# Two state space layers of a decoder: rows packed over all partitions, B and C by a block-diagonal product, half of one convolution on TensorE

## The reference

```
h = gelu(x @ w_down.T + b_down); xmid = h                     # 1024 -> 128
def _hydra(u):                                                # run twice
    zxbcdt = u @ in_w.T                                       # 256 z, 288 xBC, 8 dt
    xBC = silu(causal_conv(xBC, 7 taps) + conv_b)             # 256 xs, 16 B, 16 C
    dt_fw, dt_bw = softplus(dt[:4] + bias), softplus(flip(dt[4:]) + bias)
    y_fw = scan(x, dt_fw, A, B, C); y_bw = flip(scan(flip ...))   # 4 heads of 64, state 16
    y = shift(y_fw) + shift(y_bw) + xs * repeat(xs @ fcD_w.T + D)
    yz = y * silu(z)
    return (yz * rsqrt(mean(yz**2) + 1e-5) * norm_w) @ out_w.T
```

## Time and profile before

| | us |
|---|---|
| median of three runs | 3789.64 |
| lowest, highest | 3786.74, 3790.0 |
| the profiled execution | 3786.36 |
| its span, first to last instruction | 3784.4 |
| layer 1 in the span | 64.5 to 238.6 |
| layer 2 in the span | 238.6 to 412.6 |

### The profile page before, as it was taken

How to read it: one execution, slowest core, us unless ns; L and a number is a source line. 1 busy time by engine, 2 the same in 40 slices (tenths; PEclk the granted TensorE clock), 3 DMA queues, 4 the chain that set the end, 5 groups by cost and what they waited for, 6 DMA issues and landing times. The chain is left out here.

```text
span 3784.4 us, 106734 instructions
## 1 busy us (share of the span) xinstructions
PE 3154.1 (83%) x43205; PEld 2143.6 (57%) x43282; DVE 2080.5 (55%) x4831; ACT 1561.5 (41%) x3966; POOL 284.9 (8%) x990
## 2 busy tenths in 40 slices
PE   7555679666599999999598999999999999997698
PEld 4434255333376766666254677767666777674344
DVE  2756667677555555555221555555555555555454
ACT  2212245455322222222211566666666666663433
POOL 1000110000000000000100000000000000001232
PEclk9575889878799999999799999999999999999899
DMA  2000020200100000000101333333333333330100
GB/s 102 3 0 3 6 50 10 92 0 0 47 1 0 0 0 0 0 0 0 56 20 36 87 91 91 90 89 89 91 91 92 91 92 89 89 91 27 69 33 39
DMA packets 278662, 175.64 MB, mean 46 GB/s; under 512 B 14470, under 2 KB 267990, under 8 KB 278540
## 3 DMA queue, kind: packets, MB, share of 16 engines
q1 hardware_dynamic: 275852, 171.68, 15.4%
q0 software_dynamic: 2752, 3.18, 0.5%
HBM read 164.09 MB, written 13.90 MB: 47 GB/s over the span
## 5 line engine op out<-in xcount | busy, mean ns | idle before, releaser
L1845 PE MATMUL ps<-de_hg,st_at 128*32 128x128 f32 x16384 | 516.2, 275 | 0.3 <-DVE st_at L2007 0.3
L1845 PEld LDWEIGHTS ps<-de_hg,st_at 128*32 128x32 f32 x16384 | 424.4, 110 | 31.6 <-DVE st_at L2007 0.5
L1910 ACT ACTIVATE st_th<-ps,st_sw 128x128 f32<-128x128 f32 x1024 | 291.9, 368 | 237.2 <-PE ps L1817 237.2
L1990 DVE TENSOR_TENSOR st_th<-ps,st_sw 128x512 f32<-128x512 f32 x256 | 177.0, 692 | 163.3 <-PE ps L1817 163.3
L1257 PEld LDWEIGHTS ps<-sa_xt,w_wq 128*128 128x128 f32 x2048 | 234.1, 193 | 11.0 <-issue 9.2
L1257 PE MATMUL ps<-sa_xt,w_wq 128*128 128x128 f32 x2048 | 237.3, 277 | 1.9 <-ACT sa_xt L1373 1.9
L1328 PE MATMUL ps<-sa_wo,sa_ct 128*128 128x512 f32 x512 | 226.4, 600 | 13.2 <-issue 13.2
L1806 PE MATMUL ps<-st_hk,st_cwt 112*32 112x128 f32 x4096 | 164.7, 278 | 82.4 <-DMA st_hk<-padded_alignments 79.1
L1817 PE MATMUL ps<-st_fs,st_waf 32*128 32x128 f32 x4096 | 186.5, 296 | 16.1
L2268 PE MATMUL ps<-rf_wb,rf_sp 128*128 128x512 bf16 x737 | 175.4, 385 | 16.9 <-DVEq L2399 15.3
L1806 PEld LDWEIGHTS ps<-st_hk,st_cwt 112*32 112x32 f32 x4096 | 100.2, 109 | 147.5 <-ACT st_gt L1929 93.6
(11 more groups left out here) (384 smaller groups left out, 5911.8 us busy)
## 6 DMA issues: line engine op xcount, KB each, us to landing
st_hk<-padded_alignments SPq DMA_DIRECT2D x254, 448.0 KB, 3.6
X<-in_x_dram SPq DMA_DIRECT2D x16, 512.0 KB, 9.0
out_dram<-X SPq DMA_DIRECT2D x16, 512.0 KB, 2.7
w_wq<-in_Wq_perm_dram SPq DMA_DIRECT2D x1, 4096.0 KB
sa_wo<-in_Wo_perm_dram SPq DMA_DIRECT2D x1, 4096.0 KB, 14.4
gate_inputs<-dp_ro SPq DMA_DIRECT2D x16, 256.0 KB, 2.3
st_rin<-gate_inputs SPq DMA_DIRECT2D x128, 32.0 KB, 3.3
rf_wf<-in_weightT_dram SPq DMA_DIRECT2D x8, 512.0 KB, 8.1
```

What stands on the lines that cost most here:

```text
L1845: ins = pe.matmul(R[g][32 * q:32 * q + 32, :], at[g][:, b, :], hg[:, BG * g + b, q * P:(q + 1) * P], start=False, stop=(b == BG - 1), tile ...
L1910: ins = act.activation(th[g][:, b, :], sums(g, 0)[:, b // 2, (b % 2) * P:(b % 2 + 1) * P], ACT.Tanh, bias=sw[g][:, b:b + 1])
L1990: dve.tensor_tensor(th[g][:, 4:8, :].rearrange("p (k s) n -> p k s n", s=2), sums(g, 1).rearrange("p k (s n) -> p k s n", s=2), sw[g][:, 4 ...
```

## The change

The layer is rewritten; the result is the same function.

- dt and B/C are projected with 32 weight columns each, chunk c into partitions 32c to 32c+32 of one bank, so both occupy 128 partitions by 512 tokens. The B/C convolution reads PSUM directly; dt is copied out once, turned by four transposes, and its first two VectorE operations stand in the middle of the B/C convolution.
- The order of projection is channel tiles 0 and 1, two units of convolution, then z. `pre` holds both tiles.
- Channel tile 1: tokens 1024 to 2047 are convolved on TensorE (`convolve`), seven products per 512 tokens with `taps`, a diagonal matrix per tap; ScalarE adds the bias in its silu. VectorE convolves tokens 0 to 1023.
- B and C go to memory (4 DMAs) and come back (16 DMAs of 256 pieces of 64 bytes) as `bexp`, block-diagonal in the 8 rows of a group, and `cexp`, padded to 18 steps. One product of 18 columns per group gives C against B already reduced; the masked reduction of step 4 is gone.
- The transposes and skip sums run in chunks of 512; the skip sums, like the sums of squares, use 32 columns each at partition 32c.
- Four buffers of `pp`. The norm is done once per layer: sums of squares of the four chunks in one bank, one square root, one reciprocal, and a product with `sel` that spreads a row to all partitions. Output projections are copied to `pre` meanwhile.
- Ahead of the loop: memsets of `sel`, `bexp`, `cexp`, seven products that build `taps`, and six more small DMAs for the repeated convolution weights.

```diff
+                        for c in range(CH):
+                            sp.dma_start(dram_bc[:, c * CW:(c + 1) * CW], bc[32 * c:32 * c + 32, :]).then_inc(bc_out, 16)
+                        sp.wait_ge(bc_out, layer * 16 * CH + 16 * CH)
+                        for r in range(GRP):
+                            sp.dma_start(bexp[of, :, SEQ * r:SEQ * r + SEQ], rows[r, 0:DST], ...
+                            sp.dma_start(cexp[of, :, 1:SEQ + 1], rows[r, DST:2 * DST], ...
...
+                def convolve(pe, layer, n):
+                    pe.wait_ge(projd, layer * UNITS + 2 * CH)
+                    for d in range(TAPS):
+                        ins = pe.matmul(out[:, :, d:], taps[:, TAPS - 1 - d, :], src[:, :, 0:SEQ - d],
+                                        start=(d == 0), stop=(d == TAPS - 1))
...
-                        for g in range(NG):
-                            ins = pe.matmul(ps[:, 4, g * 8:(g + 1) * 8], u[:, g * P:(g + 1) * P], w_in[:, 544:552],
+                        for c in range(CH):
+                            pe.wait_ge(u_done, layer * CH + c + 1)
+                            ins = pe.matmul(ps[32 * c:32 * c + 32, 1, :], w_in[:, 520:552], u[:, c * CW:(c + 1) * CW],
...
+                        for n in range(2 * CH):
+                            project(pe, layer, n)
+                        for n in CONV:
+                            convolve(pe, layer, n)
...
-                            for d in range(2):
-                                ins = pe.matmul(ps[:, b, d * P:(d + 1) * P], bc[0:DST, g * P:(g + 1) * P],
+                        pe.wait_ge(bc_in, layer * 256 + 256)
+                        for g in range(NG):
+                            ins = pe.matmul(ps[:, 2, g * (SEQ + 2):(g + 1) * (SEQ + 2)], bexp[:, g, :], cexp[:, g, :],
...
                 def norm_and_out(pe, layer, c):
                     pe.wait_ge(sq_done, layer * CH + c + 1)
-                    if c >= 1:
-                        pe.wait_ge(rs_done, layer * CH + c)
-                        ins = pe.matmul(ps[:, 4, :], ones[:, :], sq[:, k, :], start=(k == 0), stop=(k == 1))
+                        ins = pe.matmul(ps[32 * c:32 * c + 32, 3, :], ones[:, 0:32], sq[:, c % 2, k, :],
...
+                        pe.wait_ge(rs_ready, layer + 1)
+                        for c in range(CH):
+                            pe.matmul(ps[:, BANK + c, :], sel[32 * c:32 * c + 32, :], rs[32 * c:32 * c + 32, :],
...
+                        for k in range(2):
+                            dve.wait_ge(projd, layer * UNITS + CH * k + CH)
+                            n = TOK >> k
+                            conv(dve, link, cv[:, k, 0:n], pre[:, k, 0:n], k)
+                        combine(dve, link, layer)
```

More of the change, by code:

```diff
@@ L301, in stage_hydra @@
+            sq = t.sb("sq", [P, 2, 2, CW])
             rs = t.sb("rs", [P, CW])
+            sel = t.sb("sel", [P, P])
+            taps = t.sb("taps", [P, TAPS, P])
             eps = t.sb("eps", [P, 1])
[L303 to L307, removed]
@@ new lines, in products @@
+                def products(pe, layer, c):
+                    for g in range(4 * c, 4 * c + 4):
+                        pe.wait_ge(p_ready, layer * NG + g + 1)
+                        if c >= 2:
+                            pe.wait_ge(y_used, layer * 2 * CH + 2 * (c - 1))
+                        for h in range(NHD):
+                            lo = HD * (h % 2)
+                            ins = pe.matmul(ps[lo:lo + HD, BANK + 2 * (c % 2) + h // 2, (g % 4) * P:(g % 4 + 1) * P],
+                                            xtok[:, g, h * HD:(h + 1) * HD], pp[:, g % 4, h, :],
+                                            start=True, stop=True)
+                        ins.then_inc(y_done, 1)
@@ L391, in _ @@
                         for c in range(CH):
[L392 to L401 removed]
+                            products(pe, layer, c)
@@ L404, in _ @@
                         norm_and_out(pe, layer, CH - 1)
+                        pe.wait_ge(rs_ready, layer + 1)
+                        for c in range(CH):
+                            pe.matmul(ps[:, BANK + c, :], sel[32 * c:32 * c + 32, :], rs[32 * c:32 * c + 32, :],
+                                      start=True, stop=True).then_inc(spread, 1)
                 @block.scalar
@@ new lines, in _ @@
+                        act.activation(cv[:, 1, 0:TOK // 2], cv[:, 1, 0:TOK // 2], ACT.Silu).then_inc(silu_done, 1)
+                        act.wait_ge(skip_sum, layer + 1)
+                        act.copy(skp[:, :], ps[:, 3, :]).then_inc(skip_kept, 1)
+                        for c in range(CH):
+                            keep_turned(1, c)
+                        act.preload_act_table(ACT.Sqrt)
+                        square(0)
+                        square(1)
+                        keep_out(0)
@@ L475, in softplus, with conv @@
                                           ALU.mult).then_inc(seg_rhs, 1)
-                def gate_and_norm(dve, link, layer, c):
+                def conv(dve, link, dst, src, tile, between=None):
+                    dv, pv = dst.rearrange("p (s t) -> p s t", t=SEQ), src.rearrange("p (s t) -> p s t", t=SEQ)
+                    link(dve.tensor_scalar(dst, src, cw[:, tile, TAPS - 1:TAPS], cb[:, tile:tile + 1], ALU.mult, ALU.add))
+                    for d in range(1, TAPS):
+                        if d == 4 and between is not None:
+                            between()
+                        ins = dve.scalar_tensor_tensor(out=dv[:, :, d:], in0=pv[:, :, 0:SEQ - d],
+                                                       scalar=cw[:, tile, TAPS - 1 - d:TAPS - d],
+                                                       in1=dv[:, :, d:], op0=ALU.mult, op1=ALU.add)
+                        if d < TAPS - 1:
+                            link(ins)
+                    ins.then_inc(conv_done, 1)
@@ new lines, in _ @@
+                        gate_rows(dve, layer, CH - 1)
+                        dve.wait_ge(rs_done, layer + 1)
+                        link(dve.reciprocal(rs[:, :], rs[:, :]))
+                        dve.sem_inc(rs_ready, 1)
+                        dve.wait_ge(o_kept, layer * CH + CH)
+                        for c in range(CH):
+                            dve.wait_ge(spread, layer * CH + c + 1)
+                            dve.tensor_tensor(u[:, c * CW:(c + 1) * CW], pre[:, 0, c * CW:(c + 1) * CW], ps[:, BANK + c, :],
+                                              ALU.mult).then_inc(u_done, 1)
```

352 lines of the change are left out of this document (197 added, 155 removed).

## The result

The changed kernel takes 3603.31 us (median of 4 runs, 3597.87 to 3605.85) where the kernel before takes 3789.82: ratio 0.9507, 95% interval 0.9491 to 0.9524. The forecast was 3611, range 3592 to 3650. The first two groups stand beside the earlier trace rows: the page's first line, then busy time by stretch (columns as there) of layer 1, of layer 2, of step 9 and of step 10 in layer 1.

A forecast was written before the change was run, and what follows sets the result against it. No engine is full; a chain passing between engines bounds the two layers. Ten steps sum to 80.9 us a layer, 169.4 for two with extras, against 348.1: 178.7 less gives 3607.7, plus 3.3 for the median 3611 us; range 3592 to 3650.

The forecast's parts named there:

- step 9: Spread, gate and norm up to the last sum of squares: 26.9 us, 3.4 of it for one norm block at 1.2 GHz.
- step 10: Norm done once per layer, with four `sel` products at 3.4 us: 7.7 us.
- step 1: Projection of dt and B/C, eight 32-column products four abreast: 1.9 us; 1.7 added once for a start at 1.2 GHz.
- hand-overs: Some thirty hand-overs of 0.1 us between engines that the steps leave out: 3.0 us over the two layers.
- step 2: Convolution of B/C on 128 partitions, its first operation from PSUM at most 0.68 us: 4.6 us together.
- no concurrency: Rival: 32-column products of dt, B/C and skip sum run singly, 2.6 us more each, 3627 us; chance 0.07.
- Step 7: Wait for the skip term after combining: 1.0 us, bounds 0 and 4, as ScalarE has copies queued ahead.
- The low clock through step 9: Rival: TensorE stays at 0.50 through spread, gate and norm, 17.7 us more a layer, 3646 us; chance 0.10.
- Prologue: New memsets and `taps` built ahead of the loop: 2.0 us.
- The read-back: B and C read back from memory: costed at nothing, slack 6 us or more, 11 ns per 64-byte piece.
- B and C late: Rival: all 4096 read-back pieces go through one DMA engine, a wait of 32.7 us a layer, 3676 us; chance 0.04.
- slower than before: Rival: read-back pieces on one DMA engine cost more, at 28 ns each a wait of 103 us, 3817 us; chance 0.01.

The follow-up runs named there:

- two_spreads: The changed kernel with two buffers for the spread masks (`pp`) instead of four: 3622.79 us, ratio 0.9554 to the kernel before.
- readback_again: The changed kernel with the 16 DMAs reading B and C back issued twice a layer, their products waiting for both: 3625.79 us, ratio 0.9573.

## Why the prediction was right, by its steps

The forecast of the profiled span was 3784.4 - 178.7 = 3605.7; it was 3601.3. The layers with their prologue took 166.6 us for 169.4 forecast (162.6 in each of the two later profiles), the part ahead of them 1.8 more, the part behind 3.4 less. That is 4.4 us of the miss of 7.7. The other 3.3 are the distance between profile and median, which this time was nil.

Layer 1 by the starts of the steps in VectorE's timeline (an ordinary table, worked out; forecast with the late clock of step 1 and without the hand-overs; the last line is summed before rounding):

| step | forecast | measured |
|---|---|---|
| 1 (dt, B/C), with 1.7 for the start | 3.6 | 3.9 |
| 2 + 3 (B/C convolution, softplus) | 14.7 | 14.5 |
| 4 (tile 0) | 12.9 | 12.8 |
| 5 (half of tile 1) | 7.1 | 7.2 |
| 6 (combining) | 5.9 | 5.9 |
| 7 (skip wait) | 1.0 | 4.9 |
| 8 (skip add) | 2.8 | 2.8 |
| 9 (spread, gate, norm) | 26.9 | 24.0 |
| 10 (norm once) | 7.7 | 6.4 |
| sum | 82.6 | 82.3 |

- *Steps 1 to 6 and 8* were right to 0.3 us in layer 1. One reading of step 2 was wrong: its first operation, from PSUM, took 0.81 us, not at most 0.68. Four products abreast took 1.06 us at full clock (L377; 2.16 at L417 in layer 1, at the lower level), which refutes *no concurrency*. In layer 2 step 1 took 4.4 us, not 1.9: its first product (151.46) starts before the last writes of `u` (to 153.20), and the clock was down. The 3.0 of hand-overs were not needed beside this.
- *Step 7*, the skip wait: 1.0 forecast, 1.5 usually measured, 4.9 once. The bounds of 0 to 4 missed the case in which the clock falls twice in TensorE's run, at the start of the convolution and behind the narrow G products. The step saw ScalarE's queue but not that it hangs on TensorE's last z unit.
- *Step 9* was charged too much: 26.9 forecast, 24.0 measured. The 3.4 us for one norm block at 1.2 GHz were not paid in any layer of the changed kernel: every norm block took 1.90 us, in layer 1 of the first profile behind a pause of 1.63 us. In layer 2 the first head products did run at the lower level (5.65 us for 4.87), at no cost to the step. *The low clock through step 9* fell with it. That a pause of 1.63 us leaves the clock up is not a rule, though: in layer 2 of two_spreads two norm blocks behind such pauses were slow. By the Trainium skill ("TensorE: Matmul & The Clock Gate", HAM oscillation) a wait between bursts of products makes the next burst start at half clock; the trace agrees for the 7.07 us wait of readback_again, and for the short pauses it shows both outcomes.
- *Step 10*: 7.7 forecast, 6.4 measured, since the four `sel` products, 32 rows deep, run abreast too: 8 instructions in 1.14 us, not 3.4. Of the 2.3 us so saved 1.0 was lost again, most of it to VectorE's first write of `u`, which stands ahead of the next layer's first product.
- *Prologue*: 2.9 us for the forecast 2.0.
- *The read-back*: its price of 11 ns a piece came out as 0.24 x 16 x 10.5 / 4096, 9.8 ns. But an issue of such a DMA takes 0.65 us for the 0.34 to 0.37 taken from another shape, 4.7 us more over sixteen. It stayed hidden: readback_again puts the slack at 4.3 to 5.3 us (6 forecast). *B and C late* and *slower than before* were far off.
- Of the signs named: VectorE busy 60 and 64 us (65), G ended at 105.3 before the half convolution (107.6), `convolve` 11.76 us (under 12), clock 1.00 in the norm blocks: all seen. `convolve` kept its 12 us only just, since 9.7 was the sum at full clock. Of the signs of being wrong one was seen as well: VectorE waited at L605 in both layers, 3.9 us more than charged in the first, which the rest of the sum made up. The rest of the span, ahead and behind together, moved by -1.6 us, within the 2 us allowed, but by +4.1 and +3.8 in the two later profiles, beyond them. The cause is open; the same program shows both. So that the forecast came within 0.2% of the time is in part luck, as is that the errors of steps 7, 9 and 10 (measured less forecast +3.9, -2.9, -1.3 us) nearly cancel in layer 1.

## What to carry to other kernels

When a chain passes between engines, add up the chain and not the busy times, and take waits of a few us from several profiles: here one of them misled a whole experiment. Sharing an operation between two engines pays until the second engine's run reaches the next thing that the first one needs, also by way of a third engine's queue. Buffers between engines must reach over whatever stands in the consumer's order, and short narrow products did best between wide ones: cut up so, the clock stayed up behind them in 4 layers of 4.

## What was not expected of the hardware

- The clock fell although TensorE was busy: behind 32 narrow instructions without a pause it was lowered in 12 layers of 18 (in ten the z projections took 5.07 to 6.55 us for 3.68, in two the transposes 3.65 for 1.97), and in none of 4 where these stood in groups of eight between wide ones.
- The same pause was followed by either clock: behind 1.92 or 1.93 us without work the convolution took 11.76 us in layer 1 and 10.06 in layer 2, in all three profiles of the changed kernel.
- Products with 32 rows run four abreast as those with 32 columns do: 8 instructions of 512 columns in 1.14 us for the one, in 1.06 for the other.
- A wait of 7 us on TensorE cost 6.3 us more behind it, through the clock.
- A DMA of SyncE that gathers 64-byte pieces took 0.65 us to issue, one of 896 pieces of another shape 0.34.
